# Products of ones beside the opening scans, two waits at seams moved, and a feed-forward product from two fp32r parts

## What is computed

```
x = x + 0.5 * ffn(layernorm(x))       # routed leaves, then one attention over 256 features
x = x + encoder(layernorm(x))         # the middle stage: 16 heads of 16 features
x = x + 0.5 * ffn(layernorm(x))

def encoder(x):
    q, k, v = x @ Wq.T + bq, x @ Wk.T + bk, x @ Wv.T + bv       # cut in 2 x 16 heads
    att = softmax(q @ k.T)                                      # 32 heads of 128 rows x 16 groups
    att_out = (att + rel_bias[buckets]) @ v
    att_block = layer_normalize(att_out @ Wo.T + bo + x)
    ff = (att_block @ W1.T + b1) @ W2.T + b2
    return layer_normalize(ff + att_block)
```

## Time and profile before

| what | us |
|---|---|
| median of 3 runs | 2936.88 (2931.88 to 2942.62) |
| the profiled execution | 2935.25 |
| its span in the trace | 2933.5 |
| PE busy | 2769.6 (94%) |
| DVE busy | 2104.6 (72%) |
| ACT busy | 1817.4 (62%) |
| POOL busy | 767.8 (26%) |
| middle stage, from its first product to the next block's first load | 704.8 to 2242.1 |

### The profile page before, as it was taken

How to read it: one execution, slowest core, us unless ns; L and a number is a source line. 1 busy time by engine, 2 the same in 40 slices (tenths; PEclk the granted TensorE clock), 3 DMA queues, 4 the chain that set the end, 5 groups by cost and what they waited for, 6 DMA issues and landing times. The chain is left out here.

```text
span 2933.5 us, 57120 instructions
## 1 busy us (share of the span) xinstructions
PE 2769.6 (94%) x21036; PEld 1714.3 (58%) x21036; DVE 2104.6 (72%) x3491; ACT 1817.4 (62%) x3539; POOL 767.8 (26%) x1202
## 2 busy tenths in 40 slices
PE   5988999997999999999999999999995699999999
PEld 2777888886733333333333333333374477788888
DVE  5545555455779999999999999999745455555544
ACT  3545433334458888888888888888865355434333
POOL 4652310001352122221222212210032653320000
PEclk8999999998869999999999999999998899999999
DMA  8994210103955545455454544534125698220110
GB/s 264 299 307 136 69 37 28 33 25 124 312 67 66 65 56 66 58 70 67 61 68 58 71 59 57 63 49 59 38 89 168 210 309 271 65 58 27 33 31 19
DMA packets 439687, 294.02 MB, mean 100 GB/s; under 512 B 163813, under 2 KB 419142, under 8 KB 439414
## 3 DMA queue, kind: packets, MB, share of 16 engines
q1 hardware_dynamic: 415222, 219.03, 36.5%
q0 software_dynamic: 24192, 71.33, 7.3%
HBM read 179.34 MB, written 114.59 MB: 100 GB/s over the span
## 5 line engine op out<-in xcount | busy, mean ns | idle before, releaser
L1590 DVE TENSOR_REDUCE mx_ha<-s_ps_ha 128x2 f32<-128x1024 f32 x1024 | 1233.5, 1214 | 66.2 <-PE s_ps_ha L1502 62.2
L1663 ACT ACTIVATE probs_ha<-s_ps_ha 128x512 f32<-128x512 f32 x2048 | 1112.3, 595 | 197.5 <-PE s_ps_ha L1514 52.8
L1502 PE MATMUL s_ps_ha<-ks_ha,qs_ha 48*128 48x512 f32 x2048 | 765.8, 455 | 4.5 <-DVE mx_ha L1590 3.0
L1514 PE MATMUL s_ps_ha<-qs_ha,ks_ha 50*128 50x512 f32 x2048 | 755.0, 449 | 0.0
L1523 PE MATMUL o_ps_ha<-probs_ha,vs_ha 128*32 128x256 f32 x8192 | 660.2, 394 | 0.4 <-ACT o_sb_ha L1655 0.4
L1502 PEld LDWEIGHTS s_ps_ha<-ks_ha,qs_ha 48*128 48x128 f32 x2048 | 309.4, 189 | 429.4 <-DVE mx_ha L1590 359.7
L907 ACT ACTIVATE probsT_a<-pT_ps_a 128x512 fp32r<-128x512 f32 x256 | 146.4, 597 | 422.2 <-PE pT_ps_a L777 422.2
L1523 PEld LDWEIGHTS o_ps_ha<-probs_ha,vs_ha 128*32 128x32 f32 x8192 | 161.8, 108 | 378.8 <-ACT probs_ha L1663 356.6
L1514 PEld LDWEIGHTS s_ps_ha<-qs_ha,ks_ha 50*128 50x128 f32 x2048 | 304.8, 186 | 11.5 <-ACT probs_ha L1663 11.1
L1463 POOL TENSOR_TENSOR onorm_ha<-oT_ha,rinv_ha 128x256 f32<-128x256 f32 x32 | 19.9, 623 | 981.4 <-DVE rinv_ha L1623 981.4
L820 DVE TENSOR_REDUCE nmax_a<-s_ps_a 128x1 f32<-128x2048 f32 x64 | 146.7, 2292 | 155.3 <-PE s_ps_a L766 155.3
(11 more groups left out here) (216 smaller groups left out, 3798.6 us busy)
## 6 DMA issues: line engine op xcount, KB each, us to landing
xs_p<-xs_d SPq DMA_DIRECT2D x282, 128.0 KB
ys_d<-y_p SPq DMA_DIRECT2D x66, 512.0 KB
qs_ha<-parts_d SPq DMA_DIRECT2D x192, 128.0 KB, 4.5
ks_ha<-parts_d SPq DMA_DIRECT2D x192, 128.0 KB, 5.1
parts_d<-parts_hp POOLq DMA_DIRECT2D x32, 512.0 KB, 5.8
xs_d<-y_p SPq DMA_DIRECT2D x6, 1024.0 KB, 12.2
leaf_w_p<-in_wa SPq DMA_DIRECT2D x4, 1048.0 KB
leaf_w_p<-in_wb SPq DMA_DIRECT2D x4, 1040.0 KB
```

The source lines that it names most:

```text
L1502: nc.tensor.matmul(s1_ps[:, e % BANKS, :], qs[0:QKROWS, k, c, :], ks[0:QKROWS, k, g * 4:(g + 1) * 4, :].rearrange("p c t -> p (c t)"), sta ...
L1514: nc.tensor.matmul(out, ks[LOW:LOW + KR, k, c, :], qs[LOW:LOW + KR, k, first:first + 4, :].rearrange("p c t -> p (c t)"), start=True, stop ...
L1590: nc.vector.reduce_max(mx[:, at:at + 2], s1_ps[:, e % BANKS:e % BANKS + 2, :], AX_X).then_inc(s1_free, 1)
L1663: nc.scalar.activation(probs[:, (RC * u + c) % (LATE + 1), 4 * g:4 * g + 4, :].rearrange("p c t -> p (c t)"), s2_ps[:, turn % TURNS, :], A ...
```

## The change

Four edits, all in the middle stage.

1. **Opening scans.** `keep_busy` is a product of ones: 64 rows of `onesr` (array rows 64 to 127) by 512 columns of ones, into `o_ps`, whose content nobody reads. One stands behind each even scan from scan 4 on and two behind each odd one: 52 scans and 78 products of ones. The wait for POOL's constants, which stood behind scan 31, now stands behind scan 3, since the ones are among the constants.
2. **Seam into `head_close`.** The wait for DVE's row of ones moves from ahead of `turn_att(0)` to `fold_row`, where the row is read.
3. **Seam out of the block.** The block is built with `no_gpsimd_drain=True`, so POOL's queue has no drain instruction at its end.
4. **Feed-forward product.** `zT` and `wff` are kept as two fp32r parts; `feed` takes 24 fp32r matmuls of 256 columns where it took 8 of fp32. ACT writes the high part with an activation (Identity) in place of a copy; DVE writes the low parts: `low_z` once a tile (128 x 1024), `low_fold` once (128 x 512). `turn_z(t)` and `feed(t)` now wait for DVE's low part (`low_set`), not for ACT's copy.

```diff
+            def keep_busy():
+                ones = onesr[LOW:P, :].rearrange("p (o c) -> p o c", o=1).broadcast_to([P - LOW, 4, P])
+                nc.tensor.matmul(o_ps[:, :], onesr[LOW:P, :], ones, start=True, stop=True)
...
-            for e in range(SCANS):
+            for e in range(BANKS):
                 scan(0, e)
             pe.wait_ge(constants_set, 4)
-            for e in range(LEAD * PAIR):
-                scan(1, e)
+            for e in range(BANKS, SCANS + LEAD * PAIR):
+                scan(e // SCANS, e % SCANS)
+                keep_busy()
+                if e % 2 == 1:
+                    keep_busy()
...
-        wff, bff, ones = sb("wff", [P, C, D]), sb("bff", [P, D]), sb("ones", [1, P])
+        wff, bff, ones = sb("wff", [P, PARTS, C, D], F32R), sb("bff", [P, D]), sb("ones", [1, P])
...
+        zT = sb("zT", [P, 2, PARTS, C, TOK], F32R)
...
+            def feed_products(t):
+                for s in range(SUB):
+                    o = mm_ps[:, 1, s // 2, (s % 2) * D:(s % 2 + 1) * D]
+                    for c in range(C):
+                        for k, (hw, hz) in enumerate(PASSES):
+                            last = nc.tensor.matmul(o, zT[:, t % 2, hz, c, s * P:(s + 1) * P], wff[:, hw, c, :],
+                                                    start=(c == 0 and k == 0), stop=(c == C - 1 and k == 2))
+                last.then_inc(f_made, 1)
...
             def turn_z(t):
                 pe.wait_ge(normed_ready, nth[0, t] + 1)
                 if t > 0:
-                    pe.wait_ge(turn_copied, made[f"z{t - 1}"])
+                    pe.wait_ge(low_set, t + 1)
...
             def feed(t):
-                pe.wait_ge(turn_copied, made["row" if t == 0 else f"z{t}"])
+                if t == 0:
+                    pe.wait_ge(turn_copied, made["row"])
+                pe.wait_ge(low_set, t + 2)
...
             def fold_row():
                 pe.wait_ge(o_copied, BLOCKS)
+                pe.wait_ge(constants_set, 1)
...
             pe.wait_ge(weights_in, FIRST_IN)
-            pe.wait_ge(constants_set, 1)
             turn_att(0)
...
-                nc.scalar.copy(dst, src).then_inc(turn_copied, 1)
+                nc.scalar.activation(dst, src, ACT.Identity).then_inc(turn_copied, 1)
...
+            def low_z(t):
+                dve.wait_ge(turn_copied, made[f"z{t}"])
+                nc.vector.tensor_tensor(zT[:, t % 2, 1], turn_ps[:, 1], zT[:, t % 2, 0].bitcast(F32), ALU.subtract).then_inc(low_set, 1)
...
                 if first in nth:
                     scales(first)
+                if step == 0:
+                    low_fold()
+                if 1 <= step <= TILES:
+                    low_z(step - 1)
                 if second in nth:
                     moments(second)
...
-            block = both.enter_context(nc.Block())
+            block = both.enter_context(nc.Block(no_gpsimd_drain=True))
```

More of the change, by code:

```diff
@@ L1726, in head_close @@
         r, z, normed, out = (sb(n, [P, k, SUB, D]) for n, k in (("r", 3), ("z", 3), ("normed", 2), ("out", 2)))
[L1727 removed]
+        attT = sb("attT", [P, 2, C, TOK])
+        zT = sb("zT", [P, 2, PARTS, C, TOK], F32R)
         stats = sb("stats", [P, SUB, 6])
@@ L1789, in _, with project_products @@
         def _(pe):
-            def token_major(lhs, rhs, bank, sem_made):
+            def project_products(t):
                 for s in range(SUB):
-                    o = mm_ps[:, bank, s // 2, (s % 2) * D:(s % 2 + 1) * D]
+                    o = mm_ps[:, 0, s // 2, (s % 2) * D:(s % 2 + 1) * D]
                     for c in range(C):
-                        last = nc.tensor.matmul(o, lhs[:, c, s * P:(s + 1) * P], rhs[:, c, :], start=(c == 0), stop=(c == C - 1))
-                last.then_inc(sem_made, 1)
+                        last = nc.tensor.matmul(o, attT[:, t % 2, c, s * P:(s + 1) * P], wo[:, c, :], start=(c == 0), stop=(c == C - 1))
+                last.then_inc(o_made, 1)
+            def feed_products(t):
[6 more added lines that the diff above has]
+                last.then_inc(f_made, 1)
             def turn_att(t):
@@ L1940, in scales, with low_fold @@
                                                ALU.mult, ALU.mult).then_inc(ln_scale, 1)
+            def low_fold():
+                dve.wait_ge(turn_copied, made["fold"])
+                nc.vector.tensor_tensor(wff[:, 1].rearrange("p c d -> p (c d)"), mm_ps[:, 1, 0, :],
+                                        wff[:, 0].rearrange("p c d -> p (c d)").bitcast(F32), ALU.subtract).then_inc(low_set, 1)
+            def low_z(t):
+                dve.wait_ge(turn_copied, made[f"z{t}"])
+                nc.vector.tensor_tensor(zT[:, t % 2, 1], turn_ps[:, 1], zT[:, t % 2, 0].bitcast(F32), ALU.subtract).then_inc(low_set, 1)
             nc.vector.memset(ones[:, :], 1.0).then_inc(constants_set, 1)
```

10 lines of the change are left out of this document (5 added, 5 removed).

## The result

| | before | changed kernel |
|---|---|---|
| median of the runs | 2934.38 us (2926.79 to 2942.62, 8 runs) | 2919.31 us (2913.36 to 2921.35, 8 runs) |
| profiled execution | 2935.25 us | 2919.09 us |
| span, mean granted clock | 2933.5 us, 0.967 | 2917.3 us, 0.978 |

The ratio is 0.9946, with a 95% interval from 0.9931 to 0.9962. The changed kernel is faster by 15 us in the medians and by 16 by the ratio, between 11 and 20. The forecast was 2917, 2.3 us from the median.

What follows compares the result with a forecast made beforehand. It took PE's half clock in unit 0, the wait into `head_close` and POOL's drain as the losses: -13.6 - 2.5 - 3.3 = -19.4, giving 2915.9 or 2917.5, forecast 2917; 8-in-10 range 2911 to 2934.

Steps and rivals of the forecast that it cites:

- The clock comes back within 4 us, and stays: Opening: products of ones bring full clock back at about 793.5; unit 0 takes 21.2 us in place of 35.3, -14.1.
- Late start +0.5: Opening: DVE's third maximum starts 2.8 us later, the faster pace cancels it, and the first score moves by +0.5 us.
- The ones lie beside the scans: Opening: a product of ones runs beside a scan; a pair takes three places, 1.32 us at half clock, 0.69 at full.
- Rival B: Opening: products of ones queue with the scans, five places or 2.2 us a pair at half clock, +22; 2956; chance 0.05.
- The fall near 790: Opening: PE stands from 786.2 to 789.6, and the clock falls at about the same place as before, 789.9.
- Lead -3.7, two thirds kept: Start of `head_close`: PE transposes 2.1 us sooner, first product 1.6 us shorter, together -3.7, of which 2.0 was counted.
- The feed-forward edit "is worth about nothing": `head_close`: DVE sets an 8.4 us step, six steps give -1.6, the last two tiles cost +1.1; -0.5 in all.
- Rivals D and E: `head_close`: D, DVE's step near 8.0, 2913; E, step 8.75, lead lost, 2921; both inside the forecast's 0.71.
- The drain -3.3: Block's end: without POOL's drain, for which all engines wait from 2238.5 to 2241.9, 3.3 us less.
- "The rest, 0.03": clock dips elsewhere: Later seams: each shifts against the clock's own pattern and may meet dips; no size given, chance 0.03.
- Rivals A and C: Opening: A, clock low when scores begin, 2934 to 2936, chance 0.13; C, clock back late, 2924 to 2930, chance 0.08.

Runs made afterwards that it cites:

- e2: Kernel before with the wait for the constants moved behind scan 3 and no products of ones: 2929.95 us, ratio 0.9992.
- e3: Kernel before with the two seam edits alone (row of ones waited for at its product, no drain of POOL): 2926.78 us, ratio 0.9979.
- e4: Kernel before with the feed-forward product in two fp32r parts alone: 2932.36 us, ratio 0.9998.
- e12: e9 with one product of ones per scan and no third one in a pair (52 in place of 78): 2922.45 us, ratio 0.9968.
- e5: Changed kernel with the tile of ones made at the block's start, so PE does not wait behind scan 3: 2916.74 us, ratio 0.9947.
- e6: Changed kernel with each product of ones on all 128 array rows: 2977.47 us, ratio 1.0154 to the kernel before.
- e7: Changed kernel without the feed-forward edit (opening, row of ones and drain only): 2913.78 us, ratio 0.9943 to the kernel before.
- e9: Changed kernel with the tile of ones made at the block's start and no feed-forward edit: 2914.77 us, ratio 0.9936 to the kernel before.
- e10: e9 with 20 bf16 products of ones ahead of the next router's first transposes: 2910.65 us, ratio 0.9921 to the kernel before.
- e8: Changed kernel with the drain of POOL at the block's end again: 2918.97 us, ratio 0.9958 to the kernel before.
- e1: Kernel before with the opening's edit alone (moved wait for the constants and 78 products of ones): 2922.80 us, ratio 0.9962.
- e11: Changed kernel with 20 products of `ident` behind each of the last two transposes of z: 2916.81 us, ratio 0.9945 to the kernel before.

## Why the prediction was right, step by step

The time and its mechanism were right: the gain is the clock in unit 0. Two terms were mis-sized, and one part of the program was left out. That the number came so near is in part luck: the change gave 2.8 us more than forecast up to the next block's load, and 6.1 went in the part behind it, which the sum did not have.

- *The clock comes back within 4 us, and stays.* It came back 6.8 us behind its fall, 2.8 later than forecast, and stayed. That it would stay was taken from a stretch in which PE was busier than in these pairs; no row had shown it. All eight kernels with three half-row places a pair, the changed one among them, show a low stretch of 3.4 or 6.8 us and 1309.8 to 1310.0 us from score to last product. The four without (before, e2, e3, e4) show 44 to 75 us, e12 47.8. The term was -14.1 and -14.8 was measured. What the prediction took as fixed, the 64.9 us, varies; the runs of e2 (10.3 shorter than before) and e3 (2.7 longer) put the loss that the change removes between 4.5 and 17.5 us.
- *Late start +0.5.* Measured +0.9 in the changed kernel, and 2.8 for the late start alone by e5. The rest was made up by the faster pace of the pairs at full clock.
- *The ones lie beside the scans.* Right, and the step on which most rests: e6, where nothing lies beside the scans, takes about 60 us more than the changed kernel. Rival B's +22 for the pairs came from five places of 0.44 us, 2.2 a pair; 3.3 us a pair was measured at low clock, which lasted through the whole opening.
- *The fall near 790.* It came, at 789.91. The idle of 3.7 us isn't its cause, at least not alone (e5); what would prevent it is open.
- *Lead -3.7, two thirds kept.* Mis-sized twice. The lead is 4.46 by e3, e7, e9, e10 and e12, and all of it is kept, also in the changed kernel: 85.57 is 0.94 under 86.51. The lead and the feed-forward edit together, -2.5 and between -5 and +1 by the prediction, measured -5.40, just outside.
- *The feed-forward edit "is worth about nothing".* Right in the sum, wrong inside. DVE's step is 8.09, near my lower bound of 8.0 rather than the 8.4 I took, since of the 0.74 of waiting for ACT only 0.27 is left. The last two tiles are where it is lost. I had priced them at +1.1. In the changed kernel, with no dip of the clock there, the last feeds start 7.42 and 6.65 us apart where it was 5.65 and 5.75, which is +2.7; the five distances before them give 3.1 back. And I had priced them without the clock. With a swing there the edit costs 1.7 to 3.1 us in the stage (e4, e5, e6); without a dip it gives 0.9 (changed kernel), with one dip it costs 0.1 (e8). Rivals D and E both fall: neither is DVE's step what decides.
- *The drain -3.3.* -3.34 in the profile. e8 shows that it is the drain's: with it back, 6.97 again. By what the Trainium skill ("VectorE: DVE Perf Modes", section "The DRAIN you can't avoid") says of boilerplate drains, about 12 ns each, it would have been 0.0; the trace, with 3.323 us for this one, decides against it.
- *"The rest, 0.03": clock dips elsewhere.* This was the step left without a price, and it took 6.1 us in the changed kernel's profile. The fourteen profiles show what it is made of. The router is short, 71.1 to 71.9 us (before, e1, e2, e10, e11), or long, 73.6 to 74.7 (the others). The clock is low from the end of `head_close`. In the short routers, e10 aside, it is full again at most 15.6 us after the load and stays so until the router's last scores. In the nine long ones it is full again 16.2 to 17.6 us after the load and dips once more for 3.4 us, as here in e9:

```profile
2206.65:2230.54 23.89, 6.39 (x16) 3.08 (x17) 8.38 (x37) 8.63 (x19) 3.10 (x2) 0.50 0.66 217
2230.54:2237.37 6.83, 4.29 (x31) 2.29 (x29) 5.21 (x21) 3.71 (x8) 3.00 (x3) 1.00 1.10 261
2237.37:2240.78 3.41, 2.88 (x10) 1.90 (x11) 1.56 (x10) 2.97 (x6) 0.96 (x1) 0.50 0.95 205
```

  The seam takes 18.9 to 19.4 us or 20.5 to 21.0, by the length of the last dips. The experts take 173.2 to 175.6, but 176.4 and 177.5 in the changed kernel and e8. In the changed kernel the longer router, experts and seam come together; the kernel before had the second shortest part of all, 691.36, against a middle value of 693.1. None of the three goes with one edit: the long router stands in kernels with the drain (e4, e8) and without, the short one too (before and e1; e11). So of the 6.1 us, 4.3 is that this profile lies above the middle value and 1.7 that the one before lies below it. What shifts the clock's changes against the work was not set by any edit here and stays open, as does why the experts took longer in two kernels.
- *Rivals A and C, the clock doesn't hold, or comes back late.* Both fell with the eight kernels above: behind the return, the clock is full in each of them to the end of `head_attend`.

One thing isn't closed. Between the first scan and the next block's load the changed kernel's profile is 22.6 us shorter than that of the kernel before, and e5, e7, e8 and e9 are 22.6, 22.3, 19.1 and 24.4 shorter; their ratios give 16, 16, 17, 12 and 19 us. That leaves 5 to 7 us. Two to three of them are the long router, which all five have and the profile of the kernel before has not. In the changed kernel the part behind the load takes back 6.1 in all, and profile and ratio agree (16.2 and 16 us). In the others something is left. The part ahead of the first scan, which the change does not touch, varies as well: 781.2 us in e7 to 787.1 in e5. And the profile of the kernel before may have a longer low stretch than its usual run. Its other runs have no profile, so that is argued, not shown.

## What to carry to other kernels

When products are added to hold the clock, place some where TensorE would stand: the two beside the scans don't do it without the third of a pair (e12), and whether the third would do without them is open. And keep them on rows that the other products leave free: on all rows they cost 60 us (e6). An edit that takes work off TensorE and gives it to a slower engine opens gaps (3.3 and 2.7 us here); price the products behind the gaps at both clocks, above all in the last tiles, where nothing else fills them. A gain of a few us at one seam can be smaller than the spread of the parts that nobody edited (6 us behind it and 6 us ahead of the first scan here): cut the profile into stretches and compare each one over several kernels before a cause is named. The version to keep is e10: ratio 0.9921 (0.9901 to 0.9940) to the kernel before, where the changed one has 0.9946 (0.9931 to 0.9962). The two intervals overlap, so its lead over the changed kernel is likely rather than certain.

## What the runs showed of the hardware that I had not expected

- The code of the opening does not fix how long the clock stays low: the same opening gave 64.9, 75.1 and 64.9 us (before, e3, e4), in kernels that differ only behind it.
- The clock can stay at 1.2 GHz for 95.6 us while the profile counts TensorE as busy for 92.6 of them. That was e6, where scans of 48 rows and products of 128 rows alternate through most of the stretch; each change between them takes 0.72 us from start to start, against 0.44 for equal ones in a row.
- The clock can fall behind a stretch in which TensorE was busy for 3.5 of 4.7 us (e5), and swing up over a gap and down under the next product (e4).
- A product of two fp32 tiles of 128 columns takes 0.23 us and two instructions; a transpose of the same tile takes 0.13.
